# Projecting the ring sum of images 3 to 6 from a high and a low part, in three rounded passes, in a fused normalise, convolve and project kernel

## The reference

```python
v = gn(x)                                   # per image and channel: (v - mean) / sqrt(var + 1e-5)
xd = concat([v[:, :, 0::2, 0::2], v[:, :, 0::2, 1::2],
             v[:, :, 1::2, 0::2], v[:, :, 1::2, 1::2]], axis=1)      # 128 channels of 32 x 32
feats = concat([dwconv(xd, w1, 1), dwconv(xd, w3, 3), dwconv(xd, w5, 5)], axis=1)   # 384 channels
y = einsum('bchw,oc->bohw', feats, w_proj[:, :, 0, 0])               # back to 128 channels
out = x + pixel_shuffle(y)                  # the four quarters of y go back to the four pixel phases
```

## Time and profile before

| | us |
|---|---|
| median of three runs | 147.66 |
| the profiled execution | 147.7 |
| its span | 145.9 |
| PE busy | 129.1 (88%) |
| DVE busy | 119.8 (82%) |
| ACT busy | 103.0 (71%) |
| POOL busy | 98.3 (67%) |
| PE's share of the chain that ended last | 85% |

### The profile page before, as it was taken

How to read it: one execution, slowest core, us unless ns; L and a number is a source line. 1 busy time by engine, 2 the same in 40 slices (tenths; PEclk the granted TensorE clock), 3 DMA queues, 4 the chain that set the end, 5 groups by cost and what they waited for, 6 DMA issues and landing times.

```text
span 145.9 us, 1480 instructions
## 1 busy us (share of the span) xinstructions
PE 129.1 (88%) x501; PEld 95.9 (66%) x501; DVE 119.8 (82%) x134; ACT 103.0 (71%) x110; POOL 98.3 (67%) x73
## 2 busy tenths in 40 slices
PE   0374699999999999999999999999999999999910
PEld 0222578788876777678767776777677867776600
DVE  0198999996299999999999999799938995999460
ACT  2285999999955999599959995999599950004100
POOL 7104799999699628994999399829993999100840
PEclk9999879999999999999999999999999999999996
DMA  3999993052043007000708699107094992853966
GB/s 101 216 210 212 209 211 50 0 110 49 0 98 57 0 19 136 0 4 17 136 0 180 122 186 206 38 17 136 0 216 84 174 198 55 180 112 85 196 145 150
DMA packets 35431, 15.73 MB, mean 108 GB/s; under 512 B 34016, under 2 KB 34144, under 8 KB 35040
## 3 DMA queue, kind: packets, MB, share of 16 engines
q1 hardware_dynamic: 33408, 8.39, 31.6%
q0 software_dynamic: 1440, 7.04, 24.9%
q10 hardware_dynamic: 576, 0.21, 0.6%
HBM read 4.41 MB, written 4.19 MB: 59 GB/s over the span
## 4 chain that ended last, share of the span: by engine, by line
PE 85%; DVE 4%; DMA 3%; ACT 2%; ACTq 1%; issue 1%; DVEq 1%; POOL 0%; POOLq 0%
PE YP L551 75%; PE YP L594 9%; DMA w_sb<-in_L_conv_w_dram 3%; DVE st L424 2%; DVE X L522 1%; ACT G L340 1%; DVE weff L449 1%; DVEq L86 0%; ACT HI L384 0%; PE SMALL L533 0%; POOL rstd L253 0%; ACTq L312 0%; ACTq L311 0%; PE SMALL L539 0%; ACTq L310 0%
## 5 line engine op out<-in xcount | busy, mean ns | idle before, releaser
L275 POOL TENSOR_TENSOR RING_SUM<-RING_SUM,PROD 128x900 f32<-128x900 f32 (+1 forms) x37 | 75.2, 2034 | 7.7 <-ACT PROD L365 3.8
L489 DVE SCALAR_TENSOR_TENSOR ACC<-G,coef,ACC 128x930 f32<-128x930 f32 (+1 forms) x64 | 76.6, 1197 | 2.0
L551 PE MATMUL YP<-HI,whi 128*128 128x512 f32 (+1 forms) x150 | 39.1, 413 | 2.8 <-ACT HI L384 2.8
L551 PE MATMUL YP<-LO,whi 128*128 128x512 f32 (+1 forms) x150 | 40.4, 420 | 0.0
L551 PE MATMUL YP<-HI,wlo 128*128 128x512 f32 (+1 forms) x150 | 37.7, 402 | 0.0
L551 PEld LDWEIGHTS YP<-HI,whi 128*128 128x128 f32 x150 | 29.5, 197 | 11.0 <-DVE whi L468 3.4
L365 ACT ACTIVATE PROD<-G,coef 128x900 f32<-128x900 f32 (+1 forms) x37 | 36.2, 1053 | 0.0
L551 PEld LDWEIGHTS YP<-LO,whi 128*128 128x128 f32 x150 | 28.5, 190 | 10.0 <-issue 3.4
L551 PEld LDWEIGHTS YP<-HI,wlo 128*128 128x128 f32 x150 | 28.3, 190 | 7.1
L375 ACT ACTIVATE Y<-YP 64x1024 f32<-64x1024 f32 x14 | 15.3, 1096 | 24.1 <-PE YP L594 23.9
L340 ACT ACTIVATE G<-X,nbias,rstd 64x1024 f32<-64x1024 f32 (+2 forms) x18 | 21.9, 1215 | 1.9 <-DVE nbias L442 1.5
(11 more groups left out here) (55 smaller groups left out, 50.3 us busy)
## 6 DMA issues: line engine op xcount, KB each, us to landing
LO<-G POOLq DMA_DIRECT2D x7, 543.0 KB, 4.9
X<-in_x_dram SPq DMA_DIRECT2D x12, 256.0 KB, 5.4
X<-Y POOLq DMA_DIRECT2D x3, 1024.0 KB, 7.0
out_dram<-X SPq DMA_DIRECT2D x12, 256.0 KB, 5.8
X<-in_x_dram SPq DMA_DIRECT2D x8, 128.0 KB, 4.3
out_dram<-X SPq DMA_DIRECT2D x8, 128.0 KB, 2.5
wp_sb<-in_L_conv_w_proj_dram ACTq DMA_DIRECT2D x1, 192.0 KB, 3.4
w_sb<-in_L_conv_w_dram ACTq DMA_DIRECT2D x1, 12.5 KB, 3.8
```

The source lines that it names most:

```text
L275: pool.tensor_tensor(dst, dst, prod(b, k), ALU.add).then_inc(prod_added, 1)
L489: dve.scalar_tensor_tensor(part(ACC, tap), g_tap(b, tap), of5(tap), part(ACC, tap), ALU.mult, ALU.add).then_inc(acc_step, 1)
L551: mm = nc.tensor.matmul(dst, w[:, n, :], src, start=start, stop=False, skip_group_check=True)
```

## The change

For images 3, 4, 5 and 6 the one float32 projection of F becomes three rounded ones, as for the inner taps: F is split into `FH`, its value rounded to float32r, and `FL = F - FH`; the weights wpT[2] likewise into `w5hi` and `w5lo`. `ring(b)` multiplies w5hi by FH, w5lo by FH and w5hi by FL, in both halves. Images 0, 1, 2 and 7 keep the float32 form.

FH is a copy on ACT: for image 3 between the second and third product of image 5, for images 4 and 5 behind the first product of image 6 and 7, for image 6 at the end, ahead of the last `copy_y`. FL is a subtraction: for images 3, 4 and 5 on DVE, behind the fourth tap (k = 3) of images 4, 5 and 6, for image 6 on POOL behind its last sum. The split of the weights is one small copy on ACT and one small subtraction on POOL at image 1.

```diff
+SPLIT_F = (3, 4, 5, 6)
+HIGH_F_AT = {(5, 1): 3, (6, 0): 4, (7, 0): 5}
+LOW_F_AT = {(4, 3): 3, (5, 3): 4, (6, 3): 5}
...
+        FH = sb("FH", [P, PH * PW], F32R)
+        FL = sb("FL", [P, PH * PW], F32R)
+        w5hi = sb("w5hi", [P, P], F32R)
+        w5lo = sb("w5lo", [P, P], F32R)
...
+            def low_f(b):
+
+                pool.wait_ge(f_high, SPLIT_F.index(b) + 1)
+                pool.tensor_tensor(FL[:, :], F[:, b % 2, :], FH[:, :].bitcast(F32), ALU.subtract).then_inc(f_low, 1)
+
             for b in range(1, B):
                 sum_ring(b)
                 if b == 1:
                     inv_std(3, 2, PAIRS)
+                    pool.wait_ge(w5hi_ready, 1)
+                    pool.tensor_tensor(w5lo[:, :], wpT[:, 2, :], w5hi[:, :].bitcast(F32),
+                                       ALU.subtract).then_inc(w5lo_ready, 1)
+            low_f(B - 2)
...
+                    if (b, k) in HIGH_F_AT:
+                        high_f(HIGH_F_AT[b, k])
...
+            def high_f(b):
+
+                act.wait_ge(f_ready, b + 1)
+                act.activation(FH[:, :], F[:, b % 2, :], ACT.Copy).then_inc(f_high, 1)
...
                 products(b)
+                if b == 1:
+                    act.activation(w5hi[:, :], wpT[:, 2, :], ACT.Copy).then_inc(w5hi_ready, 1)
             copy_y(B - 3)
+            high_f(B - 2)
             copy_y(B - 2)
...
+            def low_f(b):
+
+                dve.wait_ge(f_high, SPLIT_F.index(b) + 1)
+                dve.tensor_tensor(FL[:, :], F[:, b % 2, :], FH[:, :].bitcast(F32), ALU.subtract).then_inc(f_low, 1)
+
             for b in range(B):
                 for k in range(len(DVE_OF[b])):
                     add_tap(b, k)
+                    if (b, k) in LOW_F_AT:
+                        low_f(LOW_F_AT[b, k])
...
             def ring(b):
 
+                if b in SPLIT_F:
+                    pe.wait_ge(w5lo_ready, 1)
+                    pe.wait_ge(f_high, SPLIT_F.index(b) + 1)
+                    for w, f in ((w5hi, FH), (w5lo, FH), (w5hi, FL)):
+                        if f is FL:
+                            pe.wait_ge(f_low, SPLIT_F.index(b) + 1)
+                        for bank in range(BANKS):
+                            cols = slice(bank * 512, (bank + 1) * 512)
+                            mm = nc.tensor.matmul(YP[:, b % 2, cols], w[:, :], f[:, cols],
+                                                  start=False, stop=f is FL, skip_group_check=True)
+                    mm.then_inc(conv_done, 1)
+                    return
                 pe.wait_ge(f_ready, b + 1)
```

More of the change, by code:

```diff
@@ L152, in build @@
         last_bank = sem("last_bank")
+        f_high, f_low = sem("f_high"), sem("f_low")
+        w5hi_ready, w5lo_ready = sem("w5hi_ready"), sem("w5lo_ready")
         inner_done, conv_done, y_copied = sem("inner_done"), sem("conv_done"), sem("y_copied")
```

## The result

Before: 147.73 us, median of 6 runs. The changed kernel: 150.17 us, median of 6. The ratio is 1.0146, 95% interval 1.0106 to 1.0185: slower by 1.5%. The profiled execution took 150.34 us, its span is 148.5.

The account below looks back on a forecast made before the run. PE was taken as the bound, with DVE next. Rounded rings gain 0.28 an image, 1.12 in all, but held-up subtractions delay the last F: 147.7 + 0.4 = 148.1 us, range 146.3 to 149.3.

Parts of the forecast that it names:

- The split of the weights: Once, before image 2's sum: at most 1.07 on ACT and 0.99 on POOL, nobody waiting for it; cost nothing.
- the stepping: DVE and POOL times worked out image by image from the earlier trace, ending with F of image 7 at 137.7.
- the second toss lost: Rival: POOL's addition starts before DVE's subtraction in image 4, predicted margin 0.04; 148.7, chance 0.23.
- Held port: DVE subtractions with both inputs in SBUF and POOL's additions hold each other up for the whole length, 0.14 hidden.
- The case that all three are lost: Rival: POOL comes first at all three DVE subtractions, if DVE comes 0.2 later relative to POOL; about 149.4, chance 0.10.
- The matmuls: PE's rings of images 3 to 6: six rounded matmuls, 1.44, replace four float32 records, 1.72; gain 0.28 an image.
- ACT: Inserted copies to FH, 1.07 each in a slot of 0.95, are covered by ACT's wait of 1.69; cost nothing.
- FL of image 6 on POOL: POOL's subtraction for image 6, 2.43, falls in a stretch of 11.03 that POOL waits anyway; cost nothing.
- No contention: Rival: subtractions don't hold the port or fall into POOL's gaps, all FL are early; 146.0 to 146.7, chance 0.25.
- The end: PE reaches the last ring at 136.87, waits for F until 137.7 plus some 0.1: 0.4 later than before, giving 148.1.
- the faster case: The rival in which DVE's subtractions meet no contention, 146.0 to 146.7; chance 0.25, its lower part outside the range 0.09.

Follow-up runs that it names:

- e11: The kernel before with only the split of the weights added (small copy on ACT, small subtraction on POOL at image 1): 148.01 us.
- e12: The kernel before with one memset of four columns on POOL in the place of the weight split's subtraction: 147.94 us.
- e3: The changed kernel with POOL's first addition of images 3 and 4 waiting for DVE's first tap of images 2 and 3: 148.37 us, ratio 1.0071.
- e4: The changed kernel with all rings float32 again; FH and FL are still computed, but nobody waits for FL: 147.47 us, ratio 0.9970.
- e8: The changed kernel without DVE's three subtractions, first taps of images 2, 3 and 7 put ahead of POOL's instructions that would meet them: 145.24 us, ratio 0.9870.
- e1: The changed kernel without DVE's three subtractions, FL zeroed once by a memset on POOL: 146.67 us, ratio 0.9916.
- e6: The changed kernel with the waits of e3 and the subtractions' second input from PSUM as in e2: 146.23 us, ratio 0.9926.
- e7: The changed kernel, whole computation, with slots and waits so that instructions with two SBUF inputs avoid the other engine's additions: 146.41 us, ratio 0.9949.
- e10: The own-slots version e7 with only images 3, 4 and 6 split and image 5 in float32: 146.53 us, ratio 0.9944.
- e2: The changed kernel with the second input of DVE's three subtractions taken from ACC in PSUM instead of FH in SBUF: 148.84 us, ratio 1.0020.

## Why the prediction was wrong

- **The split of the weights: cost nothing.** This step failed. I counted its work and asked who waits for its result. But an instruction more in POOL's program moves POOL's first addition of image 3 ahead of DVE's first tap (e11, e12), and the tap takes 3.06. I had the meeting in hand: the earlier trace rows show that very tap holding that very addition, with 0.35 between their starts, and I used it as a price only. In the stepping every DVE time ahead of image 4 was taken from the trace of before as fixed. It was 2.74 late. That cost 0.75% (e3), 1.1 us by the ratios and 1.8 by the traces, most or all of the distance from 148.7, the case of the second toss lost, to 150.2.
- **Held port.** The mechanism was right in kind and size: 1.22 when free, 2.86 to 2.94 when POOL had just begun, with the 0.14 hidden that I had read from the earlier trace rows (POOL's 102.17 + 1.97, + 1.22 - 0.14 = 105.22, where FL of image 4 ends). In the order of e3, in which DVE comes on time, image 3 was free, by 0.01 and not by 0.18, and images 4 and 5 were not: the second toss, put at 0.04 us, fell to POOL, which I had as a rival at 148.7.
- **The case that all three are lost** had 149.4 and a chance of 0.10. It is nearest to what happened, though its condition, DVE 0.2 late, was 2.74: the first subtraction met only the end of an addition (1.40, 0.18 over its own time), and of PE's 1.52 all but that came from DVE being late. I took only the three subtractions as places of meeting, so no case reached 150.
- **What it feeds back.** e4 shows that the lateness of DVE costs nothing that can be told until PE waits for FL. I had the stall and POOL's shift in the stepping, one image at a time, but not that it is what makes the meetings of images 4 and 5 full ones.
- **The matmuls.** 1.37 a ring against 1.44 taken and 1.29 to 1.44 as ends: 0.35 gained an image. The Trainium skill (TensorE: Matmul & The Clock Gate, "Back-to-back issue gap") gives 216 ns for an isolated matmul of 512 columns and about 131 in a stream. Both are too low for these: two take 0.47 from 87.44 to 87.91, so 0.235 each, at a granted clock of 1.00.
- **ACT.** The inserted copies cost nothing, as said: the copies of results still start when PE lets them, and e8 has all of them and is 1.3% under before.
- **FL of image 6 on POOL: nothing.** True in the changed kernel, since DVE went straight from F of image 6 to the first tap of image 7 (127.84), while POOL had to wait for FH (128.98); false as a rule: in e1 it held that tap for 2.96.
- **No contention, 146.0 to 146.7.** The ratios of e6 and e7 make 146.6 and 146.9 of 147.7. So that rival's price was right or slightly low, and its condition wasn't met.
- **The end.** I let the time move with the last ring. The last ring starts 3.15 later than before (140.38 against 137.23), the span is 2.6 longer; and in e4 the last ring is 0.9 later and the time isn't. In the profiles ring 6 decides, whose end the first three stalls move (e10). In the forecast itself a last wait of this kind made the 0.4 over before. Had that wait been hidden, its own numbers give 147.2 as an estimate (1.12 gained, 0.6 lost by ring 6), so even with DVE on time and both tosses won 148.1 was probably high.
- **The chances** don't quite fit each other: 0.09 for the faster case under 146.3 and 0.11 for the same under 146.2.

## What to carry to other kernels

Where two engines can hold each other, list every pair of such instructions in the whole program, not just the new ones, and look at the margin between their starts: a margin of 0.35 us is lost to one more instruction somewhere ahead. Idle time of an engine hides such meetings; a change that uses the idle time up uncovers them too, so price them at the moment it is gone. And a wait that forces the order of two such instructions can be cheaper than their meeting: slots and waits turned 1.5% slower into 0.5% faster here.

## What the runs showed of the hardware

- A vector addition with both inputs in SBUF and a POOL addition exclude each other for their full length: 1.22 alone, 2.92 behind one that had just begun; POOL 1.97 alone, 2.75 behind DVE. With one input in PSUM the same subtraction took 1.22 at any time (e2, e6). This is what the Trainium skill says (SBUF — State Buffer, "shared port pair"), and the trace agrees.
- One memset of 0.09 us on POOL changed the start of an addition 14 us later by 0.35 (e12). With one more memset (e1, e8) the transfer instruction ahead of that addition started 0.33 later after its input was ready. I had not expected an instruction's place to count; the cause is open.
- A rounded matmul of 512 flat columns took 0.23 to 0.24, a float32 one 0.86 (two records of 0.43), at a granted clock of 1.00. So three rounded passes are cheaper than the float32 form by 0.35 for 1024 columns.
